# Second attention of a fused two-layer transformer kernel: preparation pieces at other points, slot 0's row ahead of the second unit's writes, and slot 1's maxima copied between two exponents

## The chip, the cores and the metric

One core of a Trainium2 chip runs the whole program. The metric is device time in microseconds (us), the median of the runs; lower is better. The core's engines run side by side, each through its own list of instructions, and meet at semaphores: PE (matrix multiply, results in PSUM), DVE, ACT and POOL (element-wise work and reductions), and SP, which here only issues DMA transfers.

## The reference, cut to what matters

The model has six stages on x (8 x 256 x 128), each behind a layer norm and added to x: a small feed-forward, an attention, the feed-forward again, a gated feed-forward with 4-bit quantisation, a second attention (L1), and the gated feed-forward once more. The change is in the second attention and in what runs beside it of the last stage.

```python
# second attention, 16 heads of width 8, causal
q_lat = jnp.einsum('bqhd,hdl->bhql', q, k_eff)
attn = jnp.einsum('bhql,bkl->bhqk', q_lat, c_kv) / sqrt(hs)
attn = jnp.where(causal[None, None], attn, -jnp.inf)
attn = jax.nn.softmax(attn, axis=-1)
y_lat = jnp.einsum('bhqk,bkl->bhql', attn, c_kv)
# last stage: each block of 16 inputs is divided by its largest magnitude / 6
# and rounded to the 4-bit grid before the product
scale = jnp.maximum(jnp.max(jnp.abs(xb), axis=-1, keepdims=True) / 6.0, 1e-12)
idx = jnp.searchsorted(_MID, jnp.abs(xb / scale))
q = _GRID[idx] * jnp.sign(xb) * scale
```

## The kernel before

**Projection.** `proj_phase` (instance `proj_b` for the second attention) makes q and k in four units of two batch rows (512 tokens). Each value is split in three bf16 parts. `sp_save` writes them to `q_dram` (L512) and `k_dram` (L516, twice): three DMAs of 192, 192 and 128 KB for each half unit. The heads are later read back from there in another order.

**Attention.** `attn_phase` works in units. A quad is two batch rows in four slots; slots 0 and 1 are the two halves of the 16 heads of the first row, slots 2 and 3 those of the second. There are four quads (the first is called quad 0), so sixteen units, written (quad, slot). For a unit:

- `sp_stack` fetches the stacks `qst`, `kst` (L644, L645): six DMAs of 96 KB.
- `pe_scores` makes a head's scores (L678 to L682 in the second attention), and `dve_max` takes the negated row maxima (L827), `dve_causal` combines them (L834).
- `pool_split` splits the maxima in three bf16 parts (L847 to L853), `pe_maxT` transposes them (L751), `act_maxT` copies them out (L804), and `sp_rows` writes them as an extra row into the stack by DMA (L656), so that the second product comes out already shifted.
- `pe_shifted` makes the shifted, transposed scores (L706, L707), two heads at a time; `act_exp` takes the exponent (L774); `pool_mask` zeroes the masked part (L786, L788); `pe_values` multiplies with the values (L725, L731); `pe_ouT` transposes (L741), `dve_norm` divides (L861, L868), `pool_x` adds to x (L881).

The units overlap: in `unit`, PE scores the unit two ahead, transposes the maxima of the unit one ahead, and makes the shifted scores and half of the values of the unit itself and the other half of the one before. The order on each engine is the order in which the functions are called; there is no planner. SP's order in a unit is the stack three units ahead and then the row one unit ahead.

**Entrance.** `entrance` joins the end of the projection and the first two units. `front(slot)` is the scoring of slots 0 and 1, with nothing to overlap. On SP, `prefetch` issues the stacks of slots 0, 1 and 2; `run(ph, 3, 4)` writes unit 1's parts (both halves); `front(0)` issues slot 0's row and slot 3's stack; then one half of unit 2's writes, slot 1's row, and the other three half units' writes. Quad 0 follows, whose unit (0,1) issues the stack of (1,0).

**Preparation pieces.** While the attention runs, the last stage's input is prepared in pieces that `in_loop` (quads 1 and 2) and `in_final` (quad 3) hang at named points of a unit: "begin", "mask1" (on POOL behind masks 0 and 1), "max1" (on DVE), "maxT" (on ACT behind the maxima's copy) and "end". They are the statistics of four tiles (`group_stats`, L1332 to L1340), 1/sqrt by power on POOL (`ln_pool`, L246), centring and scaling on ACT (`group_center` L1347, `group_scale` L1358), block maxima (`group_scales` L1365, L1368) and, for the first tiles, the rounding itself in four POOL pieces (`pool_x_scaled` L1528, `pool_x_shift` L1533, `pool_x_rounded` L1537, `pool_x_back` L1542) and one of ACT (`act_x_magic`, L1263 and L1266).

Of the kernel before, what the change touches and what calls it, by code (L numbers as in the profile page):

```python
# [58 lines left out]
def build(nc, A, out_d):  # L59
    f32, bf16, i32 = mybir.dt.float32, mybir.dt.bfloat16, mybir.dt.int32  # L60
    ALU, ACT, AX = mybir.AluOpType, mybir.ActivationFunctionType, mybir.AxisListType
# [8 lines left out]
    with ctx:  # L70
# [555 lines left out]
        def attn_phase(inst):  # L626
            l0 = inst == 0
# [34 lines left out]
                for _ in range(n):  # L662
                    nc.tensor.matmul(bank[b], identb[:], identb[:].unsqueeze(1).to_broadcast([P, 4, P]), start=True, stop=True)

            def pe_scores(pe, qd, slot, p, idle=0, b=6 if l0 else 5):

                if p == 0:
                    pe.wait_ge(sem(f"a_stack{slot}"), NSTACK * (qd + 1))
                for e in range(2):
                    h = 2 * p + e  # L670
                    wait(pe, "a_max", HH * 4 * qd + (HH * slot + h - 1))
                    ps = bank[e]
                    q, k = qst[slot][0:NQK, HEAD[h]], kst[slot][0:NQK, HEAD[h]]
                    if l0:
                        nc.tensor.matmul(ps[:, 0:S], q[:, 0:P], k[:, 0:S], start=True, stop=True)  # L675
                        last = nc.tensor.matmul(ps[:, S:2 * S], q[:, P:S], k[:, 0:S], start=True, stop=True)  # L676
                    else:
                        nc.tensor.matmul(ps[:, 0:P], q[:, 0:P], k[:, 0:P], start=True, stop=False)  # L678
                        nc.tensor.matmul(ps[:, 0:P], identb[:], maskqk[:], start=False, stop=True)  # L679
                        nc.tensor.matmul(ps[:, P:2 * P], q[:, P:S], k[:, 0:P], start=True, stop=True)  # L680
                        nc.tensor.matmul(ps[:, 2 * P:3 * P], q[:, P:S], k[:, P:S], start=True, stop=False)  # L681
                        last = nc.tensor.matmul(ps[:, 2 * P:3 * P], identb[:], maskqk[:], start=False, stop=True)  # L682
                    last.then_inc(sem("a_s"), 1)
                    pe_idle(pe, idle, b)
# [311 lines left out]
            def front(eng, which, slot):  # L996

                if l0 and slot == 0 and which in ("pe", "pool"):
                    eng.wait_ge(sem("c_masks"), 1)
                if l0 and slot == 0 and which == "pe":  # L1000
                    eng.wait_ge(sem("c_ba"), 6)
                if slot == 0:
                    if which == "pool" or which == "pe" and l0:
                        eng.wait_ge(sem("p_v"), 4 * inst + 4)
                if slot == 1 and which == "pe":
                    if not l0:
                        eng.wait_ge(sem("p_v"), 4 * inst + 4)
                    for tag in "qk":
                        eng.wait_ge(sem(f"p_{tag}r"), 4 * inst + 4)
                if which == "pe":  # L1010
                    for p in range(PR):
                        pe_scores(eng, q0, slot, p, 1)
                        if slot == 1 and p == 1:
                            pe_maxT(eng, q0, 0)
                    if slot == 1:
                        pe_shifted(eng, q0, 0, 0)
                        pe_shifted(eng, q0, 0, 1)
                        pe_maxT(eng, q0, 1)
                if which == "dve":
                    for p in range(PR):  # L1020
                        dve_max(eng, q0, slot, p)
                    if not l0:
                        dve_causal(eng, q0, slot)
                if which == "sp":
                    sp_rows(eng, q0, slot)
                    if slot == 0:
                        sp_stack(eng, q0, 3)
                if which == "act":
                    if slot == 1:
                        act_exp(eng, q0, 0, 0)  # L1030
                        act_exp(eng, q0, 0, 1)
                    act_maxT(eng, q0, slot)
                if which == "pool":
                    if slot == 0:
                        pool_vb(eng, q0, 0)
                    pool_split(eng, q0, slot)
# [112 lines left out]
        def fp4_phase(inst, nu0, x_ready, entry):  # L1149
# [225 lines left out]
            def in_loop(eng, which, qd, slot, point):  # L1375

                at = (which, slot, point)
                if at == ("dve", 1, "max1"):
                    group_stats(eng, qd)
                if at == ("pool", 1, "end"):  # L1380
                    ln_pool(eng, group(qd)[1], 0, 4)
                if at == ("act", 2, "maxT"):
                    group_center(eng, qd)
                if at == ("act", 2, "end"):
                    group_scale(eng, qd)
                if at == ("dve", 3, "max1"):
                    group_scales(eng, qd)
                if at == ("act", 3, "end"):
                    group_six(eng, qd)
                if qd == 4 * inst + 2:  # L1390
                    if at == ("pool", 0, "mask1"):
                        pool_x_scaled(eng, d0, 0)
                    if at == ("act", 0, "end"):
                        act_x_magic(eng, d0)
                    if at == ("pool", 1, "begin"):
                        pool_x_shift(eng, d0)
                    if at == ("pool", 2, "begin"):
                        pool_x_rounded(eng, d0)
                    if at == ("pool", 2, "end"):
                        pool_x_back(eng, d0, 0)  # L1400
                        pool_x_scaled(eng, d0 + 1, 1)
                    if at == ("act", 3, "maxT"):
                        act_x_magic(eng, d0 + 1)
                    if at == ("pool", 3, "end"):
                        pool_x_shift(eng, d0 + 1)

            def in_final(eng, which, slot, point):

                qd, at = 4 * inst + 3, (which, slot, point)
                if at == ("dve", 1, "max1"):  # L1410
                    group_stats(eng, qd)
                if at == ("pool", 0, "begin"):
                    pool_x_rounded(eng, d0 + 1)
                if at == ("pool", 0, "mask1"):
                    pool_x_back(eng, d0 + 1, 1)
                if at == ("pool", 0, "end"):
                    pool_x_scaled(eng, d0 + 2, 0)
                if at == ("act", 1, "maxT"):
                    act_x_magic(eng, d0 + 2)
                if at == ("pool", 1, "end"):  # L1420
                    ln_pool(eng, group(qd)[1], 0, 4)
                if at == ("pe", 2, "shifted1"):
                    eng.wait_ge(sem("a_max"), HH * 32)
                    pe_x_transpose(eng, d0, 0)
                if at == ("act", 2, "maxT"):
                    act_x_copied(eng, d0, 0)
                if at == ("act", 2, "end"):
                    group_center(eng, qd)
                if at == ("pe", 3, "begin"):
                    pe_gate(eng, d0, 0)  # L1430
                if at == ("act", 3, "end"):
                    act_silu(eng, d0)
                if at == ("pool", 3, "end"):
                    pool_x_shift(eng, d0 + 2)
                    pool_x_rounded(eng, d0 + 2)
                    pool_x_back(eng, d0 + 2, 0)
                if at == ("pe", 3, "end"):
                    eng.wait_ge(sem("a_exp"), PR * 32)
                    pe_up(eng, d0, 0)
# [366 lines left out]
        def program(eng, which):  # L1806
            def run(ph, lo, hi):
                for k in range(lo, hi):
                    step(eng, which, ph, k)
# [45 lines left out]
            def entrance(ph, at):  # L1855

                if ph is proj_a:
                    run(ph, 2, 3)
                at["prefetch"](eng, which)
                run(ph, 3, 4 if which == "sp" else 5)  # L1860
                if which in ("pe", "dve"):
                    at["front"](eng, which, 0)
                    run(ph, 5, 6)
                    at["front"](eng, which, 1)
                elif which == "sp":
                    at["front"](eng, which, 0)
                    ph["write"](eng, 2, [0])
                    at["front"](eng, which, 1)
                    ph["write"](eng, 2, [1])
                    ph["write"](eng, 3, [0, 1])  # L1870
                else:
                    run(ph, 5, 6)
                    at["front"](eng, which, 0)
                    at["front"](eng, which, 1)
# [193 lines left out]
```

## Time and profile before

| | before |
|---|---|
| median of 3 runs | 448.95 us (448.35 to 449.26) |
| the profiled execution, its own time | 450.93 us |
| its span, first to last instruction | 448.8 us |
| busy: PE, DVE, ACT, POOL | 404.5, 348.4, 286.1, 295.2 us |
| mean granted TensorE clock, share of full | 0.996 |
| PE's first score of the second attention | at 281.86 us |
| PE's last values of the second attention | end at 395.86 us |

All places in the trace are in microseconds from the start of the span. An engine's idle time costs something only where the work that follows it is on the way to the end; so the busy share tells which engine to look at, and the timeline tells where it stood. In the timeline, an idle time stands in brackets with what ended it. A row of stretches gives the busy time of each engine, the clock granted to PE (1.00 is 2.4 GHz, 0.50 is 1.2 GHz) and the transfers' share and rate.

### The profile page before, as it was taken

The page shows a single profiled execution, that of the slowest core. Times are in us where ns is not written, and L with a number is a line of the kernel's source. Part 1 is how long each engine was busy: PE and PEld are TensorE (multiplying, and loading weights), DVE is VectorE, ACT ScalarE, POOL GpSimd, SP SyncE. Part 2 cuts the span into 40 slices and gives each one's busy share as a digit, 9 for nine tenths or more (in the row PEclk, how much of TensorE's full clock was granted, in tenths as well). Part 3 has the DMA queues.
Part 4 walks back from the last instruction along what each step waited for, and adds up shares of the span by engine and source line. Part 5 has one row for each costly group of instructions (what it writes and reads, how often), then busy time and mean ns, then how long its engine had stood idle before and what let it go on. Part 6 is the DMA issues. An engine that isn't in the chain of part 4 may idle for free.

```text
span 448.8 us, 11209 instructions
## 1 busy us (share of the span) xinstructions
PE 404.5 (90%) x3802; PEld 262.1 (58%) x3802; DVE 348.4 (78%) x878; ACT 286.1 (64%) x523; POOL 295.2 (66%) x557
## 2 busy tenths in 40 slices
PE   7999789999999998888879788879999999887996
PEld 2555436666666654444457564557777777545674
DVE  5888787887878866997799987747788888277992
ACT  6785525666676676787896447226558686778641
POOL 5524646777687772346999646346787789779962
PEclk9999999999999999999999999989999999999999
DMA  7001877332324200000000006895444331000001
GB/s 219 3 0 29 211 209 216 88 106 61 100 71 98 56 4 1 2 0 2 0 2 0 1 1 156 168 239 137 108 111 105 99 82 46 6 0 1 23 25 47
DMA packets 31124, 31.82 MB, mean 71 GB/s; under 512 B 4954, under 2 KB 26330, under 8 KB 31075
## 3 DMA queue, kind: packets, MB, share of 16 engines
q1 hardware_dynamic: 31074, 31.18, 27.3%
q8 instruction: 28, 0.46, 0.4%
q14 instruction: 22, 0.17, 0.1%
HBM read 21.30 MB, written 9.44 MB: 68 GB/s over the span
## 4 chain that ended last, share of the span: by engine, by line
PE 43%; DVE 20%; POOL 18%; issue 9%; ACT 5%; DMA 3%; SPq 1%; DVEq 0%; POOLq 0%; ACTq 0%
PE psum L725 5%; POOL hq L1523 4%; DVE nm L824 4%; PE psum L675 3%; POOL hb_v L1518 2%; POOL rstd L246 2%; PE psum L706 2%; PE psum L696 2%; PE psum L676 2%; PE psum L729 2%; DVE xn L240 2%; PE psum L678 2%; PE psum L697 2%; DVE stat L224 2%; PE psum L306 2%
## 5 line engine op out<-in xcount | busy, mean ns | idle before, releaser
L774 ACT ACTIVATE h_sb<-psum 128x1024 f32<-128x1024 f32 (+1 forms) x128 | 110.6, 914 | 54.1 <-PE psum L707 27.4
L824 DVE TENSOR_REDUCE nm<-psum 128x2 f32<-128x512 f32 x128 | 81.3, 683 | 11.9 <-PE psum L676 11.3
L827 DVE TENSOR_REDUCE nm<-psum 128x3 f32<-128x384 f32 x128 | 65.6, 551 | 15.4 <-PE psum L682 14.1
L784 POOL TENSOR_TENSOR h_sb<-h_sb,bandw 128x512 f32<-128x512 f32 x45 | 57.2, 1271 | 0.0
L246 POOL TENSOR_TENSOR rstd<-veps,mhalf 128x4 f32<-128x4 f32 (+1 forms) x25 | 26.2, 1049 | 43.7 <-DVE veps L232 43.2
L725 PE MATMUL psum<-h_sb,v_b 128*32 128x256 f32 x512 | 40.9, 391 | 3.9 <-POOL h_sb L788 2.1
L788 POOL TENSOR_SCALAR_AFFINE_SELECT h_sb<-h_sb 128x512 f32<-128x512 f32 x64 | 40.7, 637 | 0.0
L675 PE MATMUL psum<-kst,qst 72*128 72x256 bf16 x128 | 33.4, 278 | 3.2 <-DMA kst<-k_dram 1.4
L676 PE MATMUL psum<-kst,qst 72*128 72x256 bf16 x128 | 32.7, 272 | 0.0
L678 PE MATMUL psum<-kst,qst 72*128 72x128 bf16 x128 | 29.1, 228 | 2.5 <-DMA kst<-k_dram 1.8
L306 PE MATMUL psum<-h_sb,dw 128*64 128x256 f32 x256 | 30.9, 385 | 0.0
L349 ACT ACTIVATE h_sb<-s_sb,pk 128x512 f32<-128x512 f32 x40 | 29.1, 802 | 0.2
L679 PE MATMUL psum<-maskqk,identb 128*128 128x128 bf16 x128 | 28.6, 223 | 0.0
L680 PE MATMUL psum<-kst,qst 72*128 72x128 bf16 x128 | 28.4, 222 | 0.0
L682 PE MATMUL psum<-maskqk,identb 128*128 128x128 bf16 x128 | 28.4, 222 | 0.0
L681 PE MATMUL psum<-kst,qst 72*128 72x128 bf16 x128 | 28.2, 220 | 0.0
L1518 POOL TENSOR_TENSOR hb_v<-hh,hb_rs 128x704 f32<-128x704 f32 x16 | 22.2, 1385 | 8.5 <-DVE hb_rs L1501 8.5
L706 PE MATMUL psum<-qst,kst 75*128 75x256 bf16 x128 | 25.0, 274 | 2.5 <-DMA qst<-nmT 2.5
L861 DVE RECIPROCAL rsum<-psum 128x16 f32<-128x16 f32 x32 | 8.2, 255 | 24.5 <-PE psum L741 24.5
L240 DVE TENSOR_SCALAR xn<-x,mv,rstd 128x128 f32<-128x128 f32 x64 | 23.0, 420 | 4.2 <-POOL rstd L246 4.0
L1211 PE MATMUL psum<-wgT,fxT 128*128 128x352 f32 x64 | 22.4, 472 | 3.8 <-ACT fxT L1283 3.8
L675 PEld LDWEIGHTS psum<-kst,qst 72*128 72x128 bf16 x128 | 12.3, 96 | 23.1 <-DVE nm L824 17.0
(256 smaller groups left out, 1144.4 us busy)
## 6 DMA issues: line engine op xcount, KB each, us to landing
qst<-q_dram SPq DMA_DIRECT2D x96, 96.0 KB
kst<-k_dram SPq DMA_DIRECT2D x96, 96.0 KB
q_dram<-q_parts SPq DMA_DIRECT2D x16, 192.0 KB, 3.0
k_dram<-k_parts SPq DMA_DIRECT2D x16, 192.0 KB, 2.9
k_dram<-k_parts SPq DMA_DIRECT2D x16, 128.0 KB, 3.2
x<-in_L_attn_x SPq DMA_DIRECT2D x4, 256.0 KB, 4.7
out_x<-x SPq DMA_DIRECT2D x4, 256.0 KB, 2.3
pk<-in_packed SPq DMA_DIRECT2D x1, 689.5 KB, 5.7
```

Source lines behind the costliest of these rows:

```text
L246: nc.gpsimd.tensor_tensor(rstd[par][:, 0:nt], veps[par][:, 0:nt], mhalf[:, 0:nt], ALU.pow).then_inc(sem("ln_rstd"), 1)
L306: last = nc.tensor.matmul(bank[gb[par]][M * half:M * half + M, 0:256], dw2[:, p], h_sb[par][:, p, 256 * half:256 * half + 256], start=(p = ...
L675: nc.tensor.matmul(ps[:, 0:S], q[:, 0:P], k[:, 0:S], start=True, stop=True)
L676: last = nc.tensor.matmul(ps[:, S:2 * S], q[:, P:S], k[:, 0:S], start=True, stop=True)
L678: nc.tensor.matmul(ps[:, 0:P], q[:, 0:P], k[:, 0:P], start=True, stop=False)
L706: nc.tensor.matmul(ps[:, 0:S], k[:, 0:P], q[:, 0:S], start=True, stop=True)
L725: nc.tensor.matmul(out[c], v[:, 0], pexp[2 * g + c // 2][:, c % 2, 0:S], start=(g == 0), stop=False)
L774: nc.scalar.activation(pexp[p][:, :, 0:w], psum[:, 4 + 2 * (p % 2):6 + 2 * (p % 2), 0:w], ACT.Exp, scale=scale).then_inc(sem("a_exp"), 1)
L784: ins = nc.gpsimd.tensor_tensor(wide, wide, bandw[:].unsqueeze(1).unsqueeze(1).to_broadcast([P, 2, 2, P]), ALU.mult)
L788: ins = nc.gpsimd.affine_select(out=diag, in_=diag, compare_op=ALU.is_ge, fill=0.0, base=0, pattern=[[0, 2], [0, 2], [1, P]], channel_mult ...
L824: nc.vector.tensor_reduce(nm[slot % 2][:, HEAD[h]], bank[e].rearrange("p (t k) -> p t k", t=2), AX.X, ALU.max, negate=True).then_inc(sem(" ...
L827: nc.vector.tensor_reduce(nm3[slot % 2][:, HEAD[h]], bank[e][:, 0:3 * P].rearrange("p (t k) -> p t k", t=3), AX.X, ALU.max, negate=True).t ...
```

## The change

At the entrance of the second attention SP leaves out `run(ph, 3, 4)`: slot 0's row and slot 3's stack are issued first, then the first half of unit 1's writes, slot 1's row, the second half of unit 1's, and units 2 and 3. PE's transpose of slot 0's maxima moves between the two heads of slot 1's second pair. ACT loads the exponent's table before slot 0's copy, by an exponent of one column. In both attentions ACT copies slot 1's maxima between the first two exponents instead of behind them.

Of the pieces: centring moves from (·,2) "maxT" to (·,1) "end" in quads 1 and 2; `ln_pool` from (·,1) "end" to (·,2) "mask1" in quads 1 to 3; the POOL pieces from "begin" and "end" to "mask1" of the same or the next unit; `act_x_magic` from "maxT" to "end". Statistics, scaling and block maxima stay.

```diff
@@ pe_scores: heads to score can be named (which=range(2))
@@ front
                     for p in range(PR):
-                        pe_scores(eng, q0, slot, p, 1)
-                        if slot == 1 and p == 1:
+                        if slot == 1 and p == 1 and not l0:
+                            pe_scores(eng, q0, slot, p, 1, which=[0])
+                            pe_maxT(eng, q0, 0)
+                            pe_scores(eng, q0, slot, p, 1, which=[1])
+                        else:
+                            pe_scores(eng, q0, slot, p, 1)
+                        if slot == 1 and p == 1 and l0:
                             pe_maxT(eng, q0, 0)
...
                 if which == "act":
+                    if slot == 0 and not l0:
+                        nc.scalar.activation(table[:], mhalf[:, 0:1], ACT.Exp)
                     if slot == 1:
                         act_exp(eng, q0, 0, 0)
+                    act_maxT(eng, q0, slot)
+                    if slot == 1:
                         act_exp(eng, q0, 0, 1)
-                    act_maxT(eng, q0, slot)
@@ in_loop
-                if at == ("pool", 1, "end"):
+                if at == ("act", 1, "end"):
+                    group_center(eng, qd)
+                if at == ("pool", 2, "mask1"):
                     ln_pool(eng, group(qd)[1], 0, 4)
-                if at == ("act", 2, "maxT"):
-                    group_center(eng, qd)
...
-                    if at == ("pool", 1, "begin"):
+                    if at == ("pool", 1, "mask1"):
                         pool_x_shift(eng, d0)
-                    if at == ("pool", 2, "begin"):
+                    if at == ("pool", 2, "mask1"):
                         pool_x_rounded(eng, d0)
-                    if at == ("pool", 2, "end"):
+                    if at == ("pool", 3, "mask1"):
                         pool_x_back(eng, d0, 0)
                         pool_x_scaled(eng, d0 + 1, 1)
-                    if at == ("act", 3, "maxT"):
+                    if at == ("act", 3, "end"):
                         act_x_magic(eng, d0 + 1)
-                    if at == ("pool", 3, "end"):
-                        pool_x_shift(eng, d0 + 1)
@@ in_final
-                if at == ("pool", 0, "begin"):
+                if at == ("pool", 0, "mask1"):
+                    pool_x_shift(eng, d0 + 1)
                     pool_x_rounded(eng, d0 + 1)
-                if at == ("pool", 0, "mask1"):
+                if at == ("pool", 1, "mask1"):
                     pool_x_back(eng, d0 + 1, 1)
-                if at == ("pool", 0, "end"):
                     pool_x_scaled(eng, d0 + 2, 0)
-                if at == ("act", 1, "maxT"):
+                if at == ("act", 1, "end"):
                     act_x_magic(eng, d0 + 2)
-                if at == ("pool", 1, "end"):
+                if at == ("pool", 2, "mask1"):
                     ln_pool(eng, group(qd)[1], 0, 4)
@@ entrance
-                run(ph, 3, 4 if which == "sp" else 5)
+                if which != "sp":
+                    run(ph, 3, 5)
+                elif ph is proj_a:
+                    run(ph, 3, 4)
...
                     at["front"](eng, which, 0)
-                    ph["write"](eng, 2, [0])
+                    if ph is proj_a:
+                        ph["write"](eng, 2, [0])
+                    else:
+                        ph["write"](eng, 1, [0])
                     at["front"](eng, which, 1)
+                    if ph is proj_b:
+                        ph["write"](eng, 1, [1])
+                        ph["write"](eng, 2, [0])
                     ph["write"](eng, 2, [1])
                     ph["write"](eng, 3, [0, 1])
```

## Rows read from the trace of the kernel before

**Rows 1.** The page: busy us (share of the span) and instructions of each engine.
```profile
PE 404.5 (90%) x3802; PEld 262.1 (58%) x3802; DVE 348.4 (78%) x878; ACT 286.1 (64%) x523; POOL 295.2 (66%) x557
```

**Rows 2.** Timeline of PE: start, us, engine, line, instruction, count, [idle before it <-what ended it].
```profile
62.60 0.28 PE L696 MATMUL psum<-qst,kst 75*128 75x256 bf16 x1 [0.28 <-DMA qst<-nmT]
...
187.53 0.66 PE L253 MATMUL psum<-ident,xn 128*128 128x128 f32 x4 [1.93 <-DVE x L875]
...
289.07 0.24 PE L751 MATMUL psum<-identb,nmb 128*48 128x128 bf16 x1
...
293.99 0.28 PE L706 MATMUL psum<-qst,kst 75*128 75x256 bf16 x1 [2.46 <-DMA qst<-nmT]
...
305.85 0.24 PE L751 MATMUL psum<-identb,nmb 128*48 128x128 bf16 x1
...
308.37 0.23 PE L678 MATMUL psum<-kst,qst 72*128 72x128 bf16 x1
...
311.87 0.24 PE L751 MATMUL psum<-identb,nmb 128*48 128x128 bf16 x1
```

**Rows 3.** Timeline of SP, which issues the DMAs.
```profile
60.33 0.77 SPq L656 DMA_DIRECT2D qst<-nmT  x1
...
284.53 5.05 SPq L516 DMA_DIRECT2D k_dram<-k_parts  x2
289.64 0.85 SPq L656 DMA_DIRECT2D qst<-nmT  x1
...
296.99 0.43 SPq L512 DMA_DIRECT2D q_dram<-q_parts  x1
...
301.56 1.06 SPq L516 DMA_DIRECT2D k_dram<-k_parts  x2
...
304.79 0.37 SPq L645 DMA_DIRECT2D kst<-k_dram  x1
```

**Rows 4.** Stretches: length, busy us of PE, PEld, DVE, ACT, POOL, PEclk, DMA share, GB/s.
```profile
290.00:293.50 3.50, 1.53 (x17) 0.77 (x14) 2.03 (x5) 0.92 (x1) 0.87 (x4) 1.00 0.91 281
293.50:298.00 4.50, 4.01 (x33) 3.09 (x34) 1.68 (x3) 1.66 (x3) 1.87 (x5) 0.72 0.90 164
297.00:298.00 1.00, 1.00 (x8) 0.72 (x7) 0.56 (x1) 0.00 (x0) 0.29 (x1) 0.50 0.76 212
298.00:304.00 6.00, 6.00 (x75) 4.39 (x74) 4.20 (x8) 2.06 (x3) 2.39 (x8) 0.93 1.03 293
304.00:307.00 3.00, 3.00 (x45) 2.29 (x45) 2.04 (x4) 2.07 (x5) 1.52 (x4) 1.00 0.76 193
```

**Rows 5.** Timeline of PE in quads 2 and 3.
```profile
361.26 0.24 PE L751 MATMUL psum<-identb,nmb 128*48 128x128 bf16 x1
...
367.40 0.24 PE L751 MATMUL psum<-identb,nmb 128*48 128x128 bf16 x1
...
369.82 0.64 PE L725 MATMUL psum<-h_sb,v_b 128*32 128x256 f32 x8 [0.62 <-POOL h_sb L788]
...
385.10 0.24 PE L751 MATMUL psum<-identb,nmb 128*48 128x128 bf16 x1
...
387.67 0.64 PE L725 MATMUL psum<-h_sb,v_b 128*32 128x256 f32 x8 [1.25 <-POOL h_sb L788]
```

**Rows 6.** Timelines of POOL and DVE; last, L1340's durations in ns (least/median/most).
```profile
293.09 0.22 POOL L853 TENSOR_TENSOR nmb<-nmr,nmb 128x16 bf16<-128x16 f32 x1
...
354.94 0.64 POOL L788 TENSOR_SCALAR_AFFINE_SELECT h_sb<-h_sb 128x512 f32<-128x512 f32 x1
...
354.98 0.62 DVE L1340 TENSOR_SCALAR veps<-mv 128x4 f32<-128x4 f32 x1
...
367.01 0.61 POOL L1542 TENSOR_TENSOR fx_q<-xb_t,xam_q 128x256 f32<-128x256 f32 x1
...
385.00 1.02 POOL L246 TENSOR_TENSOR rstd<-veps,mhalf 128x4 f32<-128x4 f32 x1
...
L1340 DVE TENSOR_SCALAR veps<-mv x3: 169/169/621, 330.5 to 381.0; 128x4 f32<-128x4 f32 x3
```

More of the change, by code:

```diff
@@ L663, in pe_idle, with pe_scores @@
                     nc.tensor.matmul(bank[b], identb[:], identb[:].unsqueeze(1).to_broadcast([P, 4, P]), start=True, stop=True)
-            def pe_scores(pe, qd, slot, p, idle=0, b=6 if l0 else 5):
+            def pe_scores(pe, qd, slot, p, idle=0, b=6 if l0 else 5, which=range(2)):
                 if p == 0:
                     pe.wait_ge(sem(f"a_stack{slot}"), NSTACK * (qd + 1))
-                for e in range(2):
+                for e in which:
                     h = 2 * p + e
@@ L1377, in in_loop @@
                 at = (which, slot, point)
+                ahead = qd == 4 * inst + 2
                 if at == ("dve", 1, "max1"):
                     group_stats(eng, qd)
-                if at == ("pool", 1, "end"):
+                if at == ("act", 1, "end"):
+                    group_center(eng, qd)
+                if at == ("pool", 2, "mask1"):
                     ln_pool(eng, group(qd)[1], 0, 4)
-                if at == ("act", 2, "maxT"):
-                    group_center(eng, qd)
                 if at == ("act", 2, "end"):
@@ L1389, in in_loop @@
                     group_six(eng, qd)
-                if qd == 4 * inst + 2:
+                if ahead:
                     if at == ("pool", 0, "mask1"):
```

## The prediction

> **What bounds the kernel now.** I read the page first, then the PE timeline of the second attention (where PE stands idle, and for whom), then SP's timeline beside it, then the traffic and the clock by stretches, and last POOL and DVE around PE's gaps. The page has PE busy for 90% of the span [rows 1]. In the second attention the reader is to see a metronome: the maxima's transpose L751, one to a unit, comes at 305.85 and 311.87, so a unit is 6.03 us of PE work with no idle row in it [rows 2]. What is lost lies in three places. (1) At the entrance PE waits 2.46 us, from 291.53 to 293.99, for slot 0's row [rows 2]. The row is issued at 289.64, while the six writes of projection unit 1 are still in the queue ahead of it: SP's second pair of L516 took 5.05 us to issue, and the traffic of 290 to 293.5 runs at 281 GB/s, the rate of the writes [rows 3, 4]. (2) After that gap the granted clock is 0.50, the 1.2 GHz level, in 297 to 298, and 0.72 over 293.5 to 298 [rows 4]. (3) Late in quads 2 and 3 PE waits 0.62 us at 369.82 and 1.25 us at 387.67, both for POOL's masks L788 [rows 5].
>
> **The change, part by part.**
>
> *The row goes ahead.* SP no longer issues unit 1's six writes before the row. PE's L751 at 289.07 [rows 2] moves ahead of one head, which takes 0.52 us of a pair's 1.1 (289.24 is the next head's start in the same timeline): the row is issued at about 289.1. In the first attention, where the queue was nearly empty, the row was issued at 60.33 and PE began with it at 62.60, 2.27 us later [rows 2, 3]. So the row is there at 291.4, and PE's scores end at 291.53: the 2.46 us wait goes. What is late next is slot 1's split: L853 runs at 293.09 for 0.22 [rows 6], set by DVE's maxima, so PE's second L751 comes at 293.35 instead of 294.75, 1.4 us earlier. Unit 0 then runs at 2.4 GHz. Its eight heads are paced by DVE at 0.55 us, and not at the 0.96 us they take at half clock (296.37 to 297.32 and on): 1.3 us more. Unit (0,1) would start 2.7 us earlier, and unit (0,2), which starts at 308.37 with no idle time [rows 2], would be reached at 305.65.
>
> *The copy between the exponents.* Slot 1's row issue goes from 296.21 to about 294.1; it is first read at unit (0,1), five us later: worth nothing by itself. The second exponent comes 0.3 us later behind it, and PE needs it only after six heads. In the first attention the same swap moves a copy at 65.07 by 0.7 us, with the row not waited for: nothing. *The early exponent table.* The load ran behind the first copy, while the row was still under way, and was over before even the new row's time: nothing saved. It now sits in the idle time ahead of that copy: nothing lost.
>
> *What those writes do now.* Unit (0,2) scores slot 0 of quad 1. Its stack is six DMAs which SP issues after every write (the last writes end at 302.62), the last at 304.79 [rows 3]. Count SP's queue in the new order: row at 289.1 (0.85), slot 3's stack (six at 0.41, 2.5), one half write (1.55), slot 1's row (0.75), then five half writes of 1.57 (L512 0.43 and the L516 pair 1.05, with gaps [rows 3]), 7.85. That is 302.6 for the end of the writes, where it was 302.62: SP had used the time before 289.6 for work that now stands behind it. The transfer engines are worse off. Before, they ran without a break from 290 to 304: writes, the stack at 164 GB/s, writes at 293 GB/s [rows 4]. Now they have only the row at 290, and the stack's first bytes come about 1 us after its issue at 290.0. All of unit 1's writes, which in part had slipped through beside the stacks in 282 to 290, come after 294.5. Six half writes of 0.52 MB at 293 to 310 GB/s are 10.2 to 10.7 us: the writes end at 304.75 and not 304.0. The stack's traffic took 3.0 us behind them (304 to 307 [rows 4]), and PE read it at 308.37. How long it had then been there no row shows: between nothing and 0.9 us (the row was read 0.5 us after the writes' traffic ended at 293.5). I take no slack: of the two ends it is the one at which a row stands, the read itself. So unit (0,2) starts at 309.0, 0.65 us later than before; bounds -0.4 (308.0, from SP's last issue at 305 and the 3 us that traffic and landing took) to +1.3 (the stack of slot 3 again at the slow 138 to 164 GB/s of the entrance).
>
> *The clock.* PE then stands idle from 305.65 to 309.0, 3.35 us. The one gap above 2 us in this trace was followed by half clock from 295.4 to 298.9; the next longest, 1.93 us at 187.53 [rows 2], was not. Half clock for those 3.4 us takes away half of what PE does in them, 1.7 us, less the part of a unit in which it waits for DVE anyway (some 0.4 of 6.03): I take 1.5; bounds 0 (the clock stays) and 1.7. Entrance in all: 0.65 + 1.5 = **+2.15 us**. The gap at 293.99 is moved, not removed, and PE's old half clock with it.
>
> *The preparation pieces.* They go from the ends and beginnings of units to the place behind masks 0 and 1, where POOL idles for exponents 2 and 3. Unit (2,3): L1542 at 367.01, 0.61 us, and L1528 of the same length behind it, 1.2 us, stand ahead of masks 0 and 1 [rows 6] and PE's values at 369.82 wait 0.62 for those masks. Behind them, the masks end at 368.4 and PE's own arrival is 369.2: -0.62. Units (1,2) and (2,2) are each 0.1 longer than 6.03 (361.26 to 367.40 is 6.14 [rows 5]); ACT's centring, 1.27 us, leaves the place ahead of exponents 2 and 3 for an idle 1.74: -0.2. In (3,0) and (3,1) the scaled piece leaves the place ahead of masks, and the sum L881, for which the statistics on DVE wait, comes some 0.2 sooner than PE's gain alone makes it: -0.2. Then (3,1): L246 at 385.00, 1.02 us [rows 6], stands between the split and the masks for which PE waits 1.25 us at 387.67; behind the masks it is in nobody's way, since masks 2 and 3 still end at about 388, before 388.3 when PE now wants them: -1.02. DVE's L834, stretched to 0.35 by a mask beside it, runs in 0.17: -0.15. Together -2.2; I take **-2.1 us**. Bounds: -0.8 (the pieces hold masks 2 and 3 and the splits instead) to -2.4. From 388 on, the gate, L774, the silu table, L1489 and POOL's tail follow in one chain, so this reaches the end in full.
>
> What I give nothing for is unit (2,1), 0.76 us over its 6.03. There L1340 took 621 ns against 169 in its other places, because it began 0.04 us after a mask L788 had begun [rows 6]. The masks there do come 0.67 us earlier now, but the moved L1533 starts where the masks end, at 354.92, and L1340 starts at 354.98, beside it. No row has a two-tensor operation of POOL beside it, so the stretch may stay whole or go: I take 0, from the row with the mask, with a bound of -0.45. The Trainium skill's rule speaks against the change at this place: SBUF — State Buffer, section "SBUF: two separate sides", says VectorE's faster modes and GpSimd share one port pair, which whoever starts first keeps for its whole instruction. By the rule the stretch stays (sum 0); without it one would credit the 0.45. The trace agrees, 621 ns against 169.
>
> **Sum.** +2.15 - 2.1 = +0.05 us. The profiled execution was 450.93 us, 448.8 of it the span and 2.1 around it; it becomes 451.0. It lies 1.98 us above the median of the runs, 448.95, so the forecast for a median is **449.0 us**. A difference under 0.2%, 0.9 us, is one that a measurement of this kernel can't tell from none.
>
> **The rivals.** *The clock stays* (26%): the wait in unit (0,2) is broken up or under 2 us, because the stack lands near 308 or PE arrives later than 305.65. For it: only one long gap has been seen, and SP alone would allow 308. Against it: 3.35 us is well above 2.46. Then 2.15 becomes 0.65 or less: 447.5, or 446.6 with the stack at 308.0. The Trainium skill, DMA: Bandwidth & Descriptors, section "Anatomy of one DMA — SWDGE (gpsimd) path", has some 2 us of fixed cost for a transfer; by that alone the last issue at 304.9 lands at 306.9 and the wait is 1.25 us. The trace does not agree: the last issue of 304.79 sent bytes until 307 with a queue ahead of it.
>
> *The stack is in time* (7%): the transfers of the entrance run fast throughout, and the 2.7 us won there are kept, with the pieces' 2.1: 444.2. Against it stands SP's count, 302.6 for the end of its writes, whatever the engines do.
>
> *Slower* (27%): the pieces hold masks 2 and 3. Place: POOL between mask 1 and mask 2 in (2,3), (3,0) and (3,1), where now 1.2, 1.75 (with v_b's copy) and 1.2 us stand. It decides once exponent 2 is ready before the pieces are done: every tenth past that delays masks 2 and 3, the split, and so L751 of the next unit. In (3,1) the split ends as L246 begins at 385.00 and L751 starts at 385.10, without slack [rows 5, 6]. If the 1.2 us show there, the -2.1 is -0.9 and the sum +1.25: 450.2; with the stack at 309.6, 450.8. For it: POOL already has no idle row before mask 2 in (3,0). Against it: ACT's magic pieces also leave the place before exponent 2, and DVE's maxima end later than the masks.
>
> **How the numbers follow.** The forecast has 40%, its own range 448.0 to 449.9; 0.03 of it falls beyond each edge of "same". Faster: 0.25 + 0.07 + 0.03 = 0.35. Same: 0.34 + 0.04 = 0.38. Slower: 0.24 + 0.03 = 0.27. The range for 8 in 10 goes from the clock staying (446.7) to the slower case with a late stack (450.8).
>
> **What would show it.** In the changed profile: no idle before L706 in slot 0, the row issued near 289.1; then an idle row of about 3 us before L678 near 309 that ends on a DMA of kst; half clock after it, and none in 295 to 299; SP's writes still ending near 302.6. No 0.62 before L725 in (2,3), under 0.3 in (3,2); L1340 in (2,1) still near 0.6. I am wrong if unit (0,2) starts before 308, if the clock stays up, or if L725 of (3,2) does not come some 2 us sooner behind the L751 of 361.26 than the 26.4 us of before.

## The result and the profile after

The changed kernel takes 454.8 us (four runs, 452.8 to 455.0) against 448.8 for the kernel before, measured beside it: ratio 1.0123, 95% interval 1.0098 to 1.0148. Repeated as e9 it gave 1.0123 again (1.0097 to 1.0149). The forecast was 449.0, "same", with a range up to 450.8: the change is slower by some 5.5 us by the ratio (5.9 by the two medians), outside the range. The profiled execution took 452.8 us (span 450.8), only 1.9 above the profiled one of before. The difference between 1.9 and 5.9 is itself one of the findings: the profiled execution of before is slower than that kernel's median, and the one of the changed kernel is the fastest of its four.

PE's busy time went up by 3.3 us against [rows 1] with the same instructions: it ran more of them at half clock.

```profile
PE 407.8 (90%) x3802; PEld 264.7 (59%) x3802; DVE 348.7 (77%) x878; ACT 287.4 (64%) x524; POOL 296.0 (66%) x557
```

PE's timeline of the changed kernel, beside [rows 2]:

```profile
272.79 0.66 PE L253 MATMUL psum<-ident,xn 128*128 128x128 f32 x4 [0.96 <-DVE xn L240]
...
287.99 0.24 PE L751 MATMUL psum<-identb,nmb 128*48 128x128 bf16 x1
...
290.89 0.27 PE L706 MATMUL psum<-qst,kst 75*128 75x256 bf16 x1
...
292.89 0.24 PE L751 MATMUL psum<-identb,nmb 128*48 128x128 bf16 x1 [1.17 <-POOL nmb L853]
...
302.64 0.24 PE L751 MATMUL psum<-identb,nmb 128*48 128x128 bf16 x1
...
309.90 0.29 PE L678 MATMUL psum<-kst,qst 72*128 72x128 bf16 x1 [4.66 <-DMA kst<-k_dram]
...
315.72 0.24 PE L751 MATMUL psum<-identb,nmb 128*48 128x128 bf16 x1
```

The row is read at 290.89 with no wait, the 2.46 us of before are gone, and unit (0,1)'s L751 comes at 302.64 where it came at 305.85. Then PE stands for 4.66 us for slot 0's next stack. Its L751 of unit (0,2) comes 13.08 us after the one before it; a plain unit takes 6.03. Of the 7.05 too many 4.66 are the wait, and the rest, 2.4, is the clock. This reading, the spacing of L751 less 6.03 and less the idle row, is how the clock is priced below.

SP of the changed kernel, beside [rows 3]:

```profile
288.56 0.77 SPq L656 DMA_DIRECT2D qst<-nmT  x1
...
291.90 0.41 SPq L512 DMA_DIRECT2D q_dram<-q_parts  x1
...
293.46 0.74 SPq L656 DMA_DIRECT2D qst<-nmT  x1
...
297.54 1.35 SPq L512 DMA_DIRECT2D q_dram<-q_parts  x1
...
302.22 1.09 SPq L516 DMA_DIRECT2D k_dram<-k_parts  x2
303.44 0.54 SPq L644 DMA_DIRECT2D qst<-q_dram  x1
...
305.66 0.37 SPq L645 DMA_DIRECT2D kst<-k_dram  x1
```

The writes end at 303.31 on this trace's clock, 302.57 on the one of before (this kernel's L253 comes 0.74 us later, 272.79 against 272.05). The L512 at 297.54 took 1.35 us and not 0.43; the stack's six issues end at 306.03.

Stretches of the changed kernel, beside [rows 4] (PEclk is the granted clock; 0.50 is the 1.2 GHz level):

```profile
290.00:293.50 3.50, 2.33 (x26) 1.58 (x24) 1.55 (x4) 1.15 (x3) 1.55 (x6) 1.00 0.67 182
293.50:298.00 4.50, 4.50 (x52) 3.14 (x50) 3.41 (x7) 1.73 (x3) 1.41 (x6) 1.00 1.04 286
298.00:304.00 6.00, 6.00 (x92) 4.49 (x89) 4.47 (x10) 3.22 (x6) 3.73 (x11) 1.00 0.95 264
304.00:307.00 3.00, 1.24 (x24) 0.69 (x21) 1.73 (x5) 0.87 (x2) 2.41 (x8) 1.00 0.79 215
...
308.50:315.20 6.70, 5.30 (x48) 4.02 (x49) 2.12 (x4) 1.72 (x3) 1.70 (x5) 0.50 0.50 84
315.30:318.30 3.00, 3.00 (x46) 2.29 (x45) 2.31 (x6) 1.86 (x4) 1.10 (x5) 1.00 0.09 25
```

The transfer engines move 182 GB/s in 290 to 293.5, where they moved 281. After the long wait the clock is 0.50 for 6.7 us, twice the stretch of before.

In quads 2 and 3, beside [rows 5], the two waits at L725 are gone. The unit from 365.05 to 371.41 is 6.36 long where 6.14 was, and the next is 6.04 where 6.71 was:

```profile
365.05 0.24 PE L751 MATMUL psum<-identb,nmb 128*48 128x128 bf16 x1
...
371.41 0.24 PE L751 MATMUL psum<-identb,nmb 128*48 128x128 bf16 x1
373.14 0.64 PE L725 MATMUL psum<-h_sb,v_b 128*32 128x256 f32 x8
...
377.45 0.24 PE L751 MATMUL psum<-identb,nmb 128*48 128x128 bf16 x1
...
389.61 0.64 PE L725 MATMUL psum<-h_sb,v_b 128*32 128x256 f32 x8
...
399.43 1.45 PE L1219 MATMUL psum<-wgT,fxT 128*128 128x352 f32 x4 [0.47 <-ACT fxT L1291]
```

From unit (0,2)'s L751 to the gate's L1219 there are 83.71 us (315.72 to 399.43). Before it was 85.63, from 311.87 [rows 2] to its own gate, L1211:

```profile
397.50 1.45 PE L1211 MATMUL psum<-wgT,fxT 128*128 128x352 f32 x4 [0.47 <-ACT fxT L1283]
```

The pieces gave **1.92 us**.

### The profile page after: what moved, and what is told of

The parts are those of the page before. It is cut to its first block, busy times and chain, and to the rows that moved or that the text cites. A ratio compares the mean times of both kernels' runs of the same rounds, so it can differ in the third digit from the quotient of the medians.

```text
span 450.8 us, 11210 instructions
## 1 busy us (share of the span) xinstructions
PE 407.8 (90%) x3802; PEld 264.7 (59%) x3802; DVE 348.7 (77%) x878; ACT 287.4 (64%) x524; POOL 296.0 (66%) x557
## 4 chain that ended last, share of the span: by engine, by line
PE 51%; DVE 16%; POOL 13%; issue 8%; ACT 6%; DMA 2%; SPq 1%; DVEq 0%; POOLq 0%; ACTq 0%
PE psum L725 6%; POOL hq L1530 4%; DVE nm L824 4%; PE psum L706 3%; PE psum L675 3%; PE psum L678 3%; ACT h_sb L349 3%; POOL hb_v L1525 2%; PE psum L696 2%; PE psum L676 2%; PE psum L729 2%; PE psum L306 2%; PE psum L697 2%; DMA kst<-k_dram 2%; PE psum L294 2%
## 5 line engine op out<-in xcount | busy, mean ns | idle before, releaser
L246 POOL TENSOR_TENSOR rstd<-veps,mhalf 128x4 f32<-128x4 f32 (+1 forms) x25 | 26.3, 1051 | 44.1 <-DVE veps L232 43.6
L725 PE MATMUL psum<-h_sb,v_b 128*32 128x256 f32 x512 | 41.3, 395 | 2.0 <-POOL h_sb L784 1.0
L678 PE MATMUL psum<-kst,qst 72*128 72x128 bf16 x128 | 29.2, 228 | 5.7 <-DMA kst<-k_dram 5.1
L786 POOL TENSOR_TENSOR gate<-mhalf 128x1 f32<-128x1 f32 x64 | 12.5, 195 | 20.7 <-ACT h_sb L774 20.7
L1219 PE MATMUL psum<-wgT,fxT 128*128 128x352 f32 x64 | 22.4, 472 | 3.8 <-ACT fxT L1291 3.8
```

Source lines behind the costliest of these rows:

```text
L725: nc.tensor.matmul(out[c], v[:, 0], pexp[2 * g + c // 2][:, c % 2, 0:S], start=(g == 0), stop=False)
```

## The experiments

Ratios are to the kernel before, measured beside each group of kernels. e5 to e8 ran on another chip than the rest, so kernels of different groups are compared by ratio, not by median. "Entrance" is the time from PE's L253 near 273 to the L751 of unit (0,2) in the profiled execution. It contains every wait of the second attention's start, and no half clock of earlier stages. Part of it is chance: PE's wait for the very first stack, at its first L678, is over before the orders differ, and was 1.45 us in before, 1.43 in e12, 0.41 in the changed kernel, 0.73 in e9, 0.90 in e8 and at most 0.52 in the others. e7's profiled execution took 452.9 us, 5 above its own median, and is left out of this column.

| kernel | ratio, 95% interval | entrance us | waits in it for slot 0's row / unit (0,2)'s stack (or row) |
|---|---|---|---|
| before | 1 | 39.82 | 2.46 / 0 |
| changed | 1.0123 (1.0098 to 1.0148) | 42.93 | 0 / 4.66 |
| e9, the same again | 1.0123 (1.0097 to 1.0149) | 43.08 | 0 / 4.35 |
| e1, SP's order as before | 0.9933 (0.9897 to 0.9968) | 36.10 | 0.23 / 0.38 |
| e2, SP's order alone | 1.0140 (1.0093 to 1.0187) | 43.30 | 0.52 / 5.40 |
| e3, stack earlier | 1.0039 (1.0008 to 1.0070) | 39.56 | 0 / 2.06 (row) |
| e4, PE kept busy | 1.0058 (1.0024 to 1.0091) | 41.21 | 0 / 1.37 |
| e5, stack and row earlier | 0.9895 (0.9844 to 0.9946) | 35.90 | 0 / 0.31 (row) |
| e6, front's small edits alone | 0.9982 (0.9954 to 1.0010) | 35.97 | 0 / 0.50 |
| e7, pieces alone | 0.9937 (0.9902 to 0.9973) | | |
| e8, as e5, one half write ahead | 0.9920 (0.9888 to 0.9952) | 36.39 | 0 / 0 |
| e10, as e5, L246 back | 0.9943 (0.9917 to 0.9970) | 36.21 | 0 / 0.16 (row) |
| e11, as e5, L1544 later | 0.9944 (0.9920 to 0.9967) | 36.04 | 0 / 0.31 (row) |
| e12, before with dummies | 1.0014 (0.9983 to 1.0045) | 39.46 | 0.41 / 2.00 |

### Which part costs: e1, e2

e1 is the changed kernel with these lines taken back, e2 the kernel before with nothing but them:

```
-                run(ph, 3, 4 if which == "sp" else 5)
+                if which != "sp":
+                    run(ph, 3, 5)
...
+                        ph["write"](eng, 1, [0])
                     at["front"](eng, which, 1)
+                    if ph is proj_b:
+                        ph["write"](eng, 1, [1])
+                        ph["write"](eng, 2, [0])
```

> The changed kernel with SP's order at the entrance of the second attention as it was before (unit 1's writes ahead of slot 0's row); the moved pieces, the earlier transpose, the table and the copy stay. Theory A (the new order makes unit (0,2)'s stack late, PE waits 4.7 us and its clock falls; the pieces are worth 1.9 us): the wait at L678 and the half clock behind it are gone, the old 2.5 us at L706 is back, and the time is 447.0 us, 0.4% under the kernel before. Theory B (the moved pieces cost time in other executions than the profiled one): over 450 us. Theory C (half clock before the attention, which this profile of the changed kernel has twice, explains the slowdown, and comes from neither edit): within 0.2% of the kernel before or like the changed kernel, by chance.

> The kernel before with nothing changed but SP's order at the entrance. Theory A: slower by the new wait and the clock less what the old gap cost, 4.0 us by the profiled pair (3.85 less the 0.74 lost ahead, and some more for what the other executions showed): 452.5 to 456.5 us. Theory B: within 0.2% of the kernel before, 448.9. Theory C: within 0.2% as well.

The order costs, the pieces gain: e1 is 0.67% faster and e2 1.40% slower. Theories B and C fall for the whole of it. e1's profile has half clock in three stretches ahead of the attention (at 55 to 58, 215 to 218 and 263 to 266) and is still 447.8 us. PE of e1, and then of e2:

```profile
274.75 0.65 PE L253 MATMUL psum<-ident,xn 128*128 128x128 f32 x4 [0.96 <-DVE xn L240]
...
293.02 0.28 PE L706 MATMUL psum<-qst,kst 75*128 75x256 bf16 x1 [0.23 <-DMA qst<-nmT]
...
304.38 0.24 PE L751 MATMUL psum<-identb,nmb 128*48 128x128 bf16 x1
...
307.35 0.23 PE L678 MATMUL psum<-kst,qst 72*128 72x128 bf16 x1 [0.38 <-DMA kst<-k_dram]
```

```profile
291.22 0.28 PE L706 MATMUL psum<-qst,kst 75*128 75x256 bf16 x1 [0.52 <-DMA qst<-nmT]
292.53 0.24 PE L751 MATMUL psum<-identb,nmb 128*48 128x128 bf16 x1 [0.48 <-POOL nmb L853]
302.29 0.24 PE L751 MATMUL psum<-identb,nmb 128*48 128x128 bf16 x1
310.28 0.29 PE L678 MATMUL psum<-kst,qst 72*128 72x128 bf16 x1 [5.40 <-DMA kst<-k_dram]
```

The surprise is e1's 0.23. With unit 1's writes ahead of the row, as before, PE did not wait 2.46 us for it. From e1's L253 to its L706 there are 18.27 us, in the profile of before 21.94. The part on the prediction comes back to it.

### The changed kernel again: e9

> The changed kernel once more, unaltered, in more runs. Its profiled execution was 452.8 us and the three others 454.7 to 455.0. Theory A: the stack's arrival in unit (0,2) varies (the wait was 4.66 us in its profile, 5.40 in e2's), and the median lies at 454.8, ratio 1.012. Rival (three runs by chance high): 452.8, ratio 1.008.

454.7 us (452.8 to 455.5): not chance. The stack arrives at the same point of the trace within 0.2 us, the wait is 4.35:

```profile
302.77 0.24 PE L751 MATMUL psum<-identb,nmb 128*48 128x128 bf16 x1
309.71 0.29 PE L678 MATMUL psum<-kst,qst 72*128 72x128 bf16 x1 [4.35 <-DMA kst<-k_dram]
315.68 0.24 PE L751 MATMUL psum<-identb,nmb 128*48 128x128 bf16 x1
```

### The clock's share: e4

```
+                    if not l0 and (qd, slot) == (q0, 2):
+                        wait(eng, "a_exp", ...)      # bank 5 is free
+                        pe_idle(eng, 19, 5)          # 19 matmuls of 512 columns, never read
```

> The changed kernel with 19 matmuls of 512 columns, which nothing reads, ahead of the wait for unit (0,2)'s stack, so that PE is busy for 4.2 of the 4.7 us. It takes the clock's part out and leaves the stack late. Theory A: unit (0,2) starts at the same time, no half clock from 308 to 315, 2.4 us less than the changed kernel: 452.4 us. Rival (the clock falls whatever PE does in the wait, or the dummies delay it as much): within 0.2% of the changed kernel's 454.8.

```profile
302.34 0.24 PE L751 MATMUL psum<-identb,nmb 128*48 128x128 bf16 x1
...
304.86 4.28 PE L663 MATMUL psum<-identb 128*128 128x512 bf16 x19
310.50 0.23 PE L678 MATMUL psum<-kst,qst 72*128 72x128 bf16 x1 [1.37 <-DMA kst<-k_dram]
...
314.01 0.24 PE L751 MATMUL psum<-identb,nmb 128*48 128x128 bf16 x1
```

The stretch 305 to 315 has PEclk 1.00, and 11.67 us between the two L751 is 6.03 and the time in which PE waited for the stack, 5.64. No clock cost is left, though the stack came 0.6 us later than in the changed kernel's profile. In the ratio e4 is 0.65% under the changed kernel, 2.9 us (1.0 to 4.8 by the two intervals): the expected 2.4 lies inside. So PE's idle time ahead of it is what brings the clock down here, and it can be bought off with useless work. The rest, e4's 0.58% (2.6 us) and the pieces' 1.9, is the late stack itself: some 4.5 us in medians.

### The place of the stack in SP's queue: e3, e5, e8

e3 issues unit (0,2)'s stack ahead of the last three half writes; it needs only element 0 of unit 1:

```
                     ph["write"](eng, 2, [0])
+                    saved(sp, 1, [0]); sp_stack(sp, q0 + 1, 0)
                     ph["write"](eng, 2, [1])
```

> The changed kernel, but SP issues the stack of unit (0,2)'s scores behind the half writes of units 1 and 2's first, ahead of the last three. Theory A: the stack is there by about 304, PE doesn't wait at L678 for slot 0's second stack, the clock stays at full, and the 2.7 us won before it are kept: the wait of 4.7 and the 2.4 of clock go, less what the three last writes do to the next stacks: 446.0 us, and at best 445. Rival (the transfer engines are the limit, whatever the order): the wait moves to the next stack, slot 1's, and the time stays above 450.

Both theories had half of it. The wait at L678 went, and a new one stood behind it, for slot 2's row, which SP issued at 307.41 behind the three writes:

```profile
304.41 0.24 PE L751 MATMUL psum<-identb,nmb 128*48 128x128 bf16 x1
309.77 0.28 PE L706 MATMUL psum<-qst,kst 75*128 75x256 bf16 x1 [2.06 <-DMA qst<-nmT]
314.11 0.24 PE L751 MATMUL psum<-identb,nmb 128*48 128x128 bf16 x1
```

The L751 are 9.70 apart: 2.06 of wait and 1.6 of half clock. 451.5 us and not 446.0. e5 takes the last half write out of the row's way too, behind slot 1's next stack:

```
-                    ph["write"](eng, 3, [0, 1])
+                    ph["write"](eng, 3, [0])       # [1]: in unit (0,2), after sp_stack
```

> As e3, with the last half write of unit 3 put behind unit (0,3)'s place in the queue's order: SP issues slot 2's row right after the fourth of five half writes, then slot 1's next stack, and only then the last half write. In e3 the row was issued at 307.41 and PE waited 2.06 us for it, with one stretch of half clock behind it (3.66 us more than a plain unit). Theory A (all of the loss is waits for SP's queue and the clock behind them): the row is issued at about 305.6, the wait is under 0.3 us, the clock stays: 447.8 us against e3's 451.5, and 445.5 where no half clock falls elsewhere. Rival (the transfers, not the queue, decide): the row or slot 1's stack is late all the same, over 450.

```profile
303.23 0.24 PE L751 MATMUL psum<-identb,nmb 128*48 128x128 bf16 x1
306.83 0.28 PE L706 MATMUL psum<-qst,kst 75*128 75x256 bf16 x1 [0.31 <-DMA qst<-nmT]
309.63 0.24 PE L751 MATMUL psum<-identb,nmb 128*48 128x128 bf16 x1
```

The row is issued at 304.23 in this profile, the wait is 0.31, and the kernel takes 445.9 us, 1.05% less than before and 2.3% less than the changed one: no write is saved, no transfer is smaller, only the order differs. The transfers as a whole are not the limit; the rival falls. e8 puts one half write back ahead of the row.

> As e5, with the first half write of unit 1 again in the idle time of SP ahead of slot 0's row, and the second behind the row. Theory A (SP's idle time before the row was a resource which the change gave up; one half write of 1.6 us fits there): row 0 on time, everything behind it 1.6 us earlier, no wait over 1 us from 280 to 320 and no half clock: 446.5 us, no slower than e5. Rival (the half write beside the stacks of slots 1 and 2 delays them as in the kernel before): a wait at the entrance comes back and it is slower than e5 by 1 us or more.

PE's L751 come at 302.56 and 308.62 (6.06 apart), with no wait for a transfer between them, and the mean granted clock of the core was 0.998, the highest of all the profiles here. The 0.90 us for which it waits for the first stack is not a price of this order: that wait ends at 281.49, and the half write is issued at 282.65. Theory A's 446.5 was met (446.7); against e5 the two can't be told apart, so SP's idle time before the row is not shown to be worth anything once the later order is right.

### The small edits and the pieces: e6, e7, e10, e11

e6 is the kernel before with `front` and `pe_scores` of the changed one; e7 is the kernel before with its `in_loop` and `in_final`.

> The kernel before with only the three small edits of the entrance: slot 0's transpose one head earlier, the exponent table at the start, slot 1's copy between the exponents. SP's order and the preparation pieces as before. Theory A (these are worth nothing by themselves, since the row is issued behind unit 1's writes anyway): within 0.2% of the kernel before. Rival (the earlier transpose brings the row, which explains that e1 waited 0.23 us at L706 and the kernel before 2.46): 0.5 to 1.5 us faster than before.

> The kernel before with only the preparation pieces at their new points. Theory A (pieces -1.9 us in the profiled pair, -2.1 forecast): 2.0 us faster than before, ratio 0.9955. Rival B (the pieces are worth less than 1 us and the entrance's small edits carried e1): within 0.2%.

e6: 0.18% less, within its interval of no change, as expected. e7: 0.63% less, 2.8 us (1.2 to 4.4), the forecast gain inside it. A sharper price is from L751 of unit (0,2) to the gate in the profiles: 85.52 us in e6 (old pieces), 83.66 in e1 (new), 1.86 apart.

```
     e10:  -  if at == ("pool", 2, "mask1"):  ln_pool      e11:  -  ("pool", 2, "mask1"): pool_x_rounded(d0)
           +  if at == ("pool", 1, "end"):    ln_pool            +  ("pool", 2, "end"):   pool_x_rounded(d0)
```

> e5 with one preparation piece back at its old point: L246, 1.02 us on POOL, behind the split of slot 1's unit in all of quads 1 to 3. The forecast had this piece alone at -1.02 (the wait for masks in (3,2)). Theory A: the wait at L725 in (3,2) is back with about 1 us, and the time is 1.0 us over e5: 446.9. Rival (masks of (3,2) are held by something else and the chain behind hides it): within 0.3 us of e5.

> e5 with POOL's rounded piece of unit (2,2) put from the place behind mask 1 to the end of the unit, so that only L246 and the copy of v stand ahead of masks 2 and 3 there. The unit took 6.35 us in every kernel with the moved pieces against 6.13 before. Theory A (the pieces hold masks 2 and 3 and so the next split in that unit alone): the 6.35 becomes 6.03 to 6.13, 0.2 to 0.3 us less than e5: 445.6. Rival (ACT's or DVE's piece in that unit sets it): 6.35 stays, within 0.1 us of e5.

PE of e10:

```profile
358.92 0.24 PE L751 MATMUL psum<-identb,nmb 128*48 128x128 bf16 x1
...
364.95 0.24 PE L751 MATMUL psum<-identb,nmb 128*48 128x128 bf16 x1
...
384.09 0.64 PE L725 MATMUL psum<-h_sb,v_b 128*32 128x256 f32 x8 [0.92 <-POOL h_sb L788]
```

L246's old place does bring the wait in (3,2) back, 0.92 us of the 1.02 forecast; but unit (2,2) falls from 6.35 to 6.03. To the gate e10 needs 84.30 us and e5 83.63: the piece is worth 0.67. The ratios can't confirm it: e10's 0.9943 is above e5's 0.9895, but so is e11's 0.9944, measured beside e10 with the piece at its new place. e11 has 6.03 in unit (2,2) as well, and 6.35 in (3,0) (371.23 to 377.58) where e5 has 6.12: 83.58 to the gate, no gain. What stands ahead of masks 2 and 3 in (2,2) of the changed kernel, POOL's timeline:

```profile
365.04 1.03 POOL L246 TENSOR_TENSOR rstd<-veps,mhalf 128x4 f32<-128x4 f32 x1
366.03 0.68 POOL L1544 TENSOR_TENSOR xb_t<-xb_t,xb_M 128x256 f32<-128x256 f32 x1
366.65 0.40 POOL L651 COPY v_b<-v_all 128x256 f32<-128x256 f32 x1
```

Together 2.0 us. Taking either of the first two away clears it: the rival "pieces hold masks 2 and 3" was real, in this unit, for 0.3 us. e11's gain there is lost again in (3,0), for a reason that no run shows, so its theory A holds for the unit and not for the time.

### The old gap: e12

```
+                        if not l0:
+                            pe_idle(eng, 6)        # slot 1, ahead of pe_shifted(eng, q0, 0, 0)
```

> The kernel before with 6 matmuls of 512 columns, which nothing reads, ahead of its wait for slot 0's row at the entrance (2.46 us in its profile, with 3.4 us of half clock behind it). Theory A (it is the idle time that brings the clock down there, 1.3 us of cost by the spacing of the heads, in the executions that have it): the wait is cut to about 1.1 us, no half clock within 295 to 299, and the median 0.3 to 1.3 us below before. Rival (most executions don't have this gap, as e1's and e6's profiles show, and the 1.3 us of dummies delay them): slower by up to 1.3 us.

Inconclusive: 1.0014, no change. Its profile has 0.41 us at L706 behind the dummies and then 2.00 for unit (0,2)'s stack, in the order of the kernel before; neither was followed by half clock within 295 to 316. The old order has no slack for that stack either: PE waits 0.38, 0.50 and 2.00 us for it in the profiles of e1, e6 and e12.

## Why the prediction was wrong

**The row and PE's lead: right, with luck in the size.** Row issued at 288.56 after the L751 of 287.99, no wait at L706, L853 and the second L751 next. Unit (0,1) comes 3.2 us earlier on the trace's clock and 3.9 earlier counted from L253; 2.7 was forecast. Most of the extra is PE's wait for slot 0's first stack, 1.45 us in the profile of before and 0.41 here:

```profile
281.86 0.23 PE L678 MATMUL psum<-kst,qst 72*128 72x128 bf16 x1 [1.45 <-DMA kst<-k_dram]
```

That wait ended before unit 1's first write was issued (282.46), so the change can't have shortened it. Only the 0.35 us for slot 1's stack, which is gone too, can be the writes' doing.

**The stack: right in place and nearly in size for this profile, in part by luck.** Forecast 309.0, measured 309.90, of which 0.74 had come before the attention (L253 at 272.79, not 272.05): +0.79 against +0.65. Counted from L253 the writes end where forecast, at 302.57 for 302.6, but by two errors that cancel: the row went out 1.3 us earlier than the counted 289.1, and the five half writes took 9.07 us and not 7.85. The count gave each of them 1.57; the trace of before already has one L512 of 1.23 us among them, at 300.29. The wait is 4.66 and not 3.35, as PE arrives 1.15 us earlier than counted and the stack 0.16 later.

**The clock: the term that was too small.** 2.4 us in the profile where 1.5 was taken, above its bound of 1.7. The step assumed that a longer wait costs the same stretch of half clock as the old one, 3.4 us; it was 6.7. e4 has the term at 2.9 us.

**The sum's base: the step that failed.** In the profiled pair the terms make up the difference: 0.74 us lost before the attention, +3.11 in the entrance (42.93 less 39.82) where +2.15 was forecast, and -1.92 for the pieces, 1.93 in all against 1.89 measured. The medians differ by 4 us more: the profile of before lies 2.1 us above its kernel's median, the changed kernel's 2.0 below its own. The sum was made against one execution of before, 450.93 us, and carried over to the median as a difference. That execution had the 2.46 us wait and the half clock behind it, and the forecast let the new wait and the new half clock replace them ("moved, not removed"). In e1, e6 and e5, where the row is in time, the entrance is 36 us long and not 39.8. e1 and e6 have SP's old order and still no such wait. The ten runs of before with a mean granted clock of 0.999 or more have a median of 447.98 us, three under the profiled one; the 22 with 0.990 to 0.994 have 449.4. So many executions of before, by their times and clocks, did not pay all that the profile shows, and had less to give back; the changed kernel pays in all three profiles that have its order (e2 and e9 among them), and its nine runs have clocks of 0.977 to 0.985. In medians the order costs 1.4% alone, 6.3 us, and 1.9% between e1 and the changed kernel, where the forecast had 2.15 us. In the profiles the changed kernel's entrance is 3.1 us longer than that of before, but 6.8 longer than e1's. The +0.65 for the late stack, the part without the clock, has the same fault. e4's two runs at a clock of 1.000 take 449.8 and 450.4 us, three of before at 1.000, measured beside them, 447.7 to 447.9. With the pieces' 1.9 taken off again, the late stack alone costs 4 us or somewhat more (an estimate; up to 0.6 of it can be e4's useless matmuls).

**The pieces: right.** -1.92 against -2.1. The waits of 0.62 and 1.25 are gone, L246's share is 0.67 net and not 1.02, and (2,2) gave back 0.2. The stretched L1348 of unit (2,1) stays, 0.65 us long at 358.74, as taken:

```profile
358.74 0.65 DVE L1348 TENSOR_SCALAR veps<-mv 128x4 f32<-128x4 f32 x1
```

POOL's moved piece had started just before it:

```profile
358.68 0.67 POOL L1540 TENSOR_TENSOR xb_t<-xb_v,xb_M 128x256 f32<-128x256 f32 x1
```

By the rule of the Trainium skill, SBUF — State Buffer, section "SBUF: two separate sides", VectorE and GpSimd share a port pair, and where both need it the one that starts first keeps it for its whole instruction; this trace agrees, with 0.65 us for L1348 beside L1540's 0.67.

Not settled: why PE reads the row 21.9 us after its L253 in the profile of before and 18.3 us after it in e1's, under the same order of SP. SP's lead over PE is not it: the first write is issued 1.2 us before that L253 in both (270.82 and 273.53). What differs is how fast the transfers run while the first stacks come in. In the 4 us that begin 6 us after L253 they moved 129 GB/s in before and 134 in e12, but 165 in e1 and 186 in e6, and PE waited 1.45, 1.43, 0.20 and 0 us for its first stack. Between the entrances of before and e1, 3.7 us apart, stand 1.6 us of waits for the stacks of slots 0 and 1 and 2.2 of the wait for the row; the other differences cancel. No run set that rate on purpose, and the kernel before was profiled only once. So that its long entrance is an execution's own and not the kernel's habit rests on the times and clocks of its other runs, and on e1 and e6; e12's entrance, the order of before with useless matmuls, was long as well (39.46).

## What to carry to other kernels

When a short urgent transfer is moved ahead of bulk writes, ask which later transfer now stands behind all of them, and move that one too: the order of e5 won 2.3% over the changed kernel, by their ratios, with the same transfers. Before a wait of the profile is booked as a cost that the change takes away or displaces, look whether the profiled execution is above the median; if it is, its wait may be its own, and the new one everybody's. Preparation pieces fit behind a mask as long as together they end before the next exponent does: here 1.2 us of them cost nothing in unit (2,3), and 2.0 us cost 0.3 in (2,2).

## What the hardware showed

- The clock after a wait: 2.46 us of idle PE was followed by 3.4 us at the 1.2 GHz level, 4.66 us by 6.7 us, of which 1.4 lay in the wait itself; e3's 2.06 cost 1.6 us in the same way, while 2.00 in e12 was not followed by any. A gap of 1.94 us near 187 was followed by half clock (189 to 192.4) in the changed kernel's profile; one of 1.93 at the same place in the profile of before was not.
- 19 useless matmuls of 4.28 us in all kept the clock at 1.00 and saved some 2.9 us (1.0 to 4.8) in medians; the profiled pair has 2.4 us of clock cost to save.
- SP's issue of a write's first transfer, 0.41 to 0.50 us as a rule, took longer once in the middle of the writes: 1.35 us in the changed kernel (297.54), 1.47 in e9, 1.43 in e4, 1.23 in before (300.29), 1.98 in e12.
- Under the same order of transfers, the rate behind L253 was 129 GB/s in one execution (before) and 165 in another (e1), with 1.6 us less of waiting for the first two stacks.
